# Attention that projects raw rows: the layer norm's mean in the weights, its scale in the factors, X rescaled in place

## What is computed

```python
x = x + 0.5 * ffn(layernorm(x))
a = layernorm(x)
q, k, v = split(rms_norm(a) @ w_qkv.T)
w = exp(rms_norm(k))
y = sigmoid(rms_norm(q)) * cumsum(w * v) / (cumsum(w) + 1e-6)
u, g = split(y @ w_swiglu.T)
x = x + a + (u * silu(g)) @ w_out.T
x = x + 0.5 * ffn(layernorm(x))
```

## Time and profile before

| what | us |
|---|---|
| median of 3 runs (lowest, highest) | 782.3 (782.26, 782.41) |
| span of the profiled execution | 859.9 |
| the profiled execution's time around its span | not shown by the page |
| attention, from the last shared sum to the last add_attention, in the profile | 386.5 to 508.0 |
| busy in the span: PE, DVE, ACT, POOL | 717.7, 447.1, 348.5, 427.7 |

### The profile page before, as it was taken

One profiled execution on the slowest core, in us unless ns is written; L12 is line 12 of the kernel. 1 busy time (PEld: TensorE's weight loads), 2 busy tenths in 40 slices (PEclk: granted clock), 3 DMA queues, 4 the chain that ended last, 5 costly groups with the idle time before them and its releaser, 6 DMA issues.

```text
span 859.9 us, 12865 instructions
## 1 busy us (share of the span) xinstructions
PE 717.7 (83%) x4282; PEld 591.9 (69%) x4282; DVE 447.1 (52%) x1089; ACT 348.5 (41%) x913; POOL 427.7 (50%) x499
## 2 busy tenths in 40 slices
PE   3863998988888988985887687998998988888996
PEld 3742877877776767873565475786876777777874
DVE  7689743323233333425999977953333332323437
ACT  3622622323333233445775535831333332323433
POOL 6439052465555646347898524033365656555430
PEclk9985898999999999997999997998999999999999
DMA  9600010111111111021110010001111111111128
GB/s 317 230 1 0 1 37 17 30 43 37 40 38 37 42 34 44 25 85 58 40 39 24 26 50 0 2 25 25 28 41 35 43 34 43 37 40 36 31 71 247
DMA packets 45021, 43.75 MB, mean 51 GB/s; under 512 B 5984, under 2 KB 39776, under 8 KB 44576
## 3 DMA queue, kind: packets, MB, share of 16 engines
q1 hardware_dynamic: 35872, 24.32, 9.2%
q0 software_dynamic: 9088, 18.63, 7.8%
HBM read 27.33 MB, written 15.60 MB: 50 GB/s over the span
## 4 chain that ended last, share of the span: by engine, by line
issue 40%; PE 36%; DVE 8%; ACT 3%; another core or an unknown queue 2%; DMA 1%; SPq 0%; POOL 0%; DVEq 0%; ACTq 0%
PE psY L1463 8%; PE psH L1446 4%; PE psH L1375 3%; PE psG L1306 3%; PE psG L1304 2%; PE psG L1305 2%; PE psU L1306 2%; PE psU L1304 2%; PE psU L1305 2%; DVE rec L1045 1%; PE psG L1529 1%; PE psU L1562 1%; ACT silu L1190 1%; PE psT L1403 1%
## 5 line engine op out<-in xcount | busy, mean ns | idle before, releaser
L638 POOL DMA_INDIRECT results<-yout,target x142 | 139.7, 984 | 182.3 <-DVE yout L949 144.2
L745 DVE TENSOR_TENSOR hr<-silu,psU 128x512 f32<-128x512 f32 x142 | 97.3, 685 | 252.2 <-ACT silu L1190 129.4
L623 POOL DMA_INDIRECT rows<-tokens,source x142 | 137.0, 965 | 137.8 <-issue 69.0
L1463 PE MATMUL psY<-W,hT 128*128 x1120 | 152.6, 279 | 18.2 <-issue 12.2
L1190 ACT ACTIVATE silu<-psG 128x512 f32<-128x512 f32 x142 | 85.1, 599 | 203.6 <-PE psG L1306 148.7
L1463 PEld LDWEIGHTS psY<-W,hT 128*128 128x128 f32 x1120 | 135.9, 192 | 29.6 <-issue 22.9
L1183 ACT ACTIVATE hT<-psH 128x512 f32<-128x512 f32 x142 | 84.7, 596 | 110.5 <-remote 57.2
L1446 PE MATMUL psH<-ident,hr 128*128 128x128 f32 x568 | 86.4, 275 | 26.4 <-DVE hr L745 26.4
L1446 PEld LDWEIGHTS psH<-ident,hr 128*128 128x128 f32 x568 | 68.6, 141 | 53.2 <-DVE hr L745 37.8
L745 DVE TENSOR_TENSOR hs<-silu,psU 128x512 f32<-128x512 f32 x64 | 43.4, 683 | 59.0 <-PE psU L1306 30.8
L1375 PEld LDWEIGHTS psH<-W2S,hs 128*128 128x128 f32 x512 | 65.9, 210 | 8.1 <-DVE hs L745 6.9
(11 more groups left out here) (187 smaller groups left out, 1266.1 us busy)
## 6 DMA issues: line engine op xcount, KB each, us to landing
W<-w_e SPq DMA_DIRECT2D x3, 2048.0 KB, 13.4
tokens<-XN SPq DMA_DIRECT2D x16, 256.0 KB, 3.1
Y<-results SPq DMA_DIRECT2D x32, 128.0 KB, 2.3
YF<-results SPq DMA_DIRECT2D x16, 256.0 KB, 5.1
rows<-tokens,source POOLq DMA_INDIRECT x142
results<-yout,target POOLq DMA_INDIRECT x142
X<-x SPq DMA_DIRECT2D x8, 256.0 KB, 5.6
out<-X SPq DMA_DIRECT2D x8, 256.0 KB, 2.6
```

The lines of the kernel that those rows point to most:

```text
L623: pool.indirect_dma_start(rows[:, g % RING, t, :], None, tokens, bass.IndirectOffsetOnAxis(ap=source[:, tile:tile + 1], axis=0))\
L638: pool.indirect_dma_start(results, bass.IndirectOffsetOnAxis(ap=target[:, tile:tile + 1], axis=0), yout[:, g % 2, t, :], None).then_inc(y_ ...
L745: dve.tensor_tensor(hidden, silu[:, s.u % 2, :], psU[:, s.u % 2, :], ALU.mult).then_inc(h_done, 1)
L1463: i = pe.matmul(into[:, t * D:(t + 1) * D], hT[:, s.u % 2, f, :], W2[:, bass.ds(at + f * D, D)], start=(f == 0), stop=(f == FT - 1))
```

## The change

PE transposes X itself and not `xn`. For this the qkv weights are centred once: DVE makes `centre` = identity - 1/128, PE multiplies it with WQKV into PSUM, ACT copies the product back into WQKV. The rows' scale cancels out of q and k through their norms' terms and enters v through `at_fac`. POOL's power works on eight columns; the last two give rstd, from which it makes `at_scale` = 1 + rstd and `at_shift` = mean * rstd. DVE rescales X in place (X * at_scale - at_shift = x + a), after PE's transpose of it. at_rsqrt, mean_square, residual and at_normalise are gone. The lags behind the projection fall by two.

```diff
-POOL_STAGES = [("qkv_rsqrt", 5), ("residual", 5), ("at_rsqrt", 3), ("mean_square", 4), ("add_routed", 1)]
-DVE_STAGES = [("at_normalise", 4), ("at_aggregate", 3), ("gate_g", 8), ("at_statistics", 2), ("gate_u", 8),
-              ("invert", 6), ("scale_q", 6), ("weigh_v", 5), ("attend", 6), ("add_attention", 9)]
-ACT_STAGES = [("tanh_g", 8), ("gate_results", 0), ("denominator", 6), ("copy_yT", 7), ("copy_anT", 4),
-              ("weights", 5), ("squares", 4)]
-PE_STAGES = [("cumulate", 6), ("transpose_y", 7), ("project", 9), ("transpose_xn", 4), ("qkv", 4),
-             ("swiglu", 7)]
+POOL_STAGES = [("scale_eps", 3), ("qkv_rsqrt", 3), ("add_routed", 1)]
+DVE_STAGES = [("rescale", 4), ("at_aggregate", 3), ("gate_g", 6), ("at_statistics", 2), ("gate_u", 6),
+              ("invert", 4), ("scale_q", 4), ("weigh_v", 3), ("attend", 4), ("add_attention", 7)]
+ACT_STAGES = [("tanh_g", 6), ("gate_results", 0), ("denominator", 4), ("copy_yT", 5), ("copy_xT", 2),
+              ("weights", 3), ("squares", 2)]
+PE_STAGES = [("cumulate", 4), ("transpose_y", 5), ("project", 7), ("transpose_x", 2), ("qkv", 2),
+             ("swiglu", 5)]
...
-TURNED_STEP = {20: (0, 1), 21: (2,), 22: (3,), 23: (4,), 24: (5,)}
+TURNED_STEP = {18: (0, 1), 19: (2,), 20: (3,), 21: (4,), 22: (5,)}
...
+                def scale_eps(s):
                     pool.wait_ge(at_stat, s.i + 1)
+                    u = s.u % 2
                     pool.tensor_tensor(at_eps[:, u, :, :], at_ms[:, u, 2, :].unsqueeze(1).to_broadcast([P, 2, TB]),
                                        rms_eps[:, :, :], ALU.mult).then_inc(rms_terms, 1)
...
                 def qkv_rsqrt(s):
                     pool.wait_ge(ss_done, s.i + 1)
                     pool.wait_ge(rms_terms, s.i + 1)
                     if s.past(2):
                         pool.wait_ge(kv_done, s.i - 1)
+                        pool.wait_ge(x_scaled, s.i - 1)
...
-                    pool.tensor_tensor(at_fac[:, s.u % 2, :, :], ms, minus_half[:, 0:3 * TB]
-                                       .rearrange("p (a t) -> p a t", a=3), ALU.pow).then_inc(qk_scaled, 1)
+                    pool.tensor_tensor(at_fac[:, u, :, :], ms, minus_half[:, 0:4 * TB]
+                                       .rearrange("p (a t) -> p a t", a=4), ALU.pow).then_inc(qk_scaled, 1)
+                    pool.wait_ge(qk_scaled, s.i + 1)
+                    pool.tensor_tensor(at_scale[:, u, :], at_fac[:, u, 3, :], ones[:, 0:TB], ALU.add)
+                    pool.tensor_tensor(at_shift[:, u, :], at_mv[:, u, :, 0], at_fac[:, u, 3, :], ALU.mult)\
+                        .then_inc(at_scaled, 1)
...
                 add_shared(CHUNKS - 1)
+                dve.scalar_tensor_tensor(centre[:, :], ones[:, :], -1.0 / D, ident[:, :], ALU.mult, ALU.add)\
+                   .then_inc(centre_made, 1)
...
-                def at_normalise(s):
+                def rescale(s):
                     dve.wait_ge(at_scaled, s.i + 1)
-                    if s.past(2):
-                        dve.wait_ge(anT_psum, s.i - 1)
-                        dve.wait_ge(xres_done, s.i - 1)
+                    dve.wait_ge(anT_psum, s.i + 1)
                     for t in range(TB):
...
+                        xt = X[:, s.i * TB + t, :]
+                        i = dve.tensor_scalar(xt, xt, at_scale[:, s.u, t:t + 1], at_shift[:, s.u, t:t + 1],
+                                              ALU.mult, ALU.subtract)
+                    i.then_inc(x_scaled, 1)
...
+                act.wait_ge(centred_psum, 1)
+                act.activation(WQKV[:, :], psU[:, 0, 0:3 * D], ACT.Copy).then_inc(centred, 1)
                 act_end = BATCHES + max(d for _, d in ACT_STAGES)
                 pipelined(act, [(stages[n], d) for n, d in ACT_STAGES], BATCHES, 4, straight=True,
...
+                pe.wait_ge(centre_made, 1)
+                pe.wait_ge(h_done, shared_at(0, SHARED - 1) + 1)
+                pe.matmul(psU[:, 0, 0:3 * D], centre[:, :], WQKV[:, :], start=True, stop=True)\
+                  .then_inc(centred_psum, 1)
+                pe.wait_ge(centred, 1)
...
-                    pe.wait_ge(xn_ready, s.i + 1)
+                    pe.wait_ge(routed_added, s.i + 1)
...
-                        i = pe.transpose(psT[:, t * P:(t + 1) * P], xn[:, s.u, t, :], ident[:, :])
+                        i = pe.transpose(psT[:, t * P:(t + 1) * P], X[:, s.i * TB + t, :], ident[:, :])
```

More of the change, by code:

```diff
@@ L249, in macaron @@
         at_mv = sb("at_mv", [P, 2, TB, 2])
-        at_var = sb("at_var", [P, 2, 2, TB])
-        at_rstd = sb("at_rstd", [P, 2, TB])
-        at_sq = sb("at_sq", [P, 2, TB])
+        at_scale = sb("at_scale", [P, 2, TB])
+        at_shift = sb("at_shift", [P, 2, TB])
         at_eps = sb("at_eps", [P, 2, 2, TB])
-        at_ms = sb("at_ms", [P, 2, 3, TB])
-        at_fac = sb("at_fac", [P, 2, 3, TB])
+        at_ms = sb("at_ms", [P, 2, 4, TB])
+        at_fac = sb("at_fac", [P, 2, 4, TB])
         qk_ss = sb("qk_ss", [P, 2, 2, TB])
@@ L304, in macaron @@
         memory = overlaid(
-            [("xn", [P, 2, TB, D], fp32),
+            [("centre", [P, P], fp32),
              ("anT", [P, 2, TB * P], fp32),
@@ L319, in macaron @@
             [("XNTL", [P, NT], fp32r), ("XNTH", [P, NT], fp32r)])
-        xn = memory["xn"]
+        centre = memory["centre"]
         anT = memory["anT"]
@@ L413, in macaron @@
         at_stat = sem("at_stat")
-        sq_link = sem("sq_link")
         rms_terms = sem("rms_terms")
         at_scaled = sem("at_scaled")
-        xn_ready = sem("xn_ready")
-        xres_done = sem("xres_done")
+        x_scaled = sem("x_scaled")
+        centre_made = sem("centre_made")
+        centred_psum = sem("centred_psum")
+        centred = sem("centred")
         anT_psum = sem("anT_psum")
@@ L682, in qkv_rsqrt @@
                         pool.wait_ge(kv_done, s.i - 1)
-                    ms = at_ms[:, s.u % 2, :, :]
-                    pool.tensor_tensor(ms[:, 0:2, :], qk_ss[:, s.u % 2, :, :], at_eps[:, s.u % 2, :, :], ALU.add)\
+                        pool.wait_ge(x_scaled, s.i - 1)
+                    u = s.u % 2
+                    ms = at_ms[:, u, :, :]
+                    pool.tensor_tensor(ms[:, 0:2, :], qk_ss[:, u, :, :], at_eps[:, u, :, :], ALU.add)\
                         .then_inc(qk_link, 1)
                     pool.wait_ge(qk_link, s.i + 1)
-                    pool.tensor_tensor(at_fac[:, s.u % 2, :, :], ms, minus_half[:, 0:3 * TB]
-                                       .rearrange("p (a t) -> p a t", a=3), ALU.pow).then_inc(qk_scaled, 1)
+                    pool.tensor_tensor(at_fac[:, u, :, :], ms, minus_half[:, 0:4 * TB]
[4 more added lines that the diff above has]
+                        .then_inc(at_scaled, 1)
                 if l == 0:
-                    stages = {"qkv_rsqrt": qkv_rsqrt, "add_routed": add_routed, "residual": residual,
-                              "at_rsqrt": at_rsqrt, "mean_square": mean_square}
+                    stages = {"qkv_rsqrt": qkv_rsqrt, "add_routed": add_routed, "scale_eps": scale_eps}
                     def scale_ahead(chunks):
@@ L1080, in _ @@
                 stages = {"weigh_v": weigh_v, "gate_u": gate_u, "add_attention": add_attention,
-                          "at_normalise": at_normalise, "at_statistics": at_statistics, "attend": attend,
+                          "at_statistics": at_statistics, "attend": attend, "rescale": rescale,
                           "at_aggregate": at_aggregate, "invert": invert, "scale_q": scale_q, "gate_g": gate_g}
```

45 lines of the change are left out of this document (12 added, 33 removed).

## The result

The changed kernel takes 788.5 us (median of 7 runs, 784.0 to 789.2). The kernel before, run beside it, takes 782.3 us (7 runs, 780.8 to 783.6). The ratio is 1.0068, 95% interval 1.0045 to 1.0091: slower by 5.3 us (0.0068 x 782.3; interval 3.5 to 7.1). The medians differ by 6.2, since the changed kernel's runs lie in two groups, two near 784.0 and five from 788.4 to 789.2. The forecast was 786.8, the range 781.9 to 790.0, and "slower" had 0.74. Sign and range held. The parts did not all: the start had the wrong sign, and PE's low clock in the last steps, which costs 2.4 to 4.2 us by the profiles, had no term; the two made up for each other in part.

What follows compares the result with a forecast made beforehand. DVE was taken as full in attention's middle (busy 44.0 of 45.7 us), POOL and gating as off the path. Start 1.5, lost cover 1.0 and POOL's path 2.0 gave +4.5 us: 786.8 us, range 781.9 to 790.0.

Steps and rivals of the forecast that it cites:

- (a): Start of attention: ACT's copy of the centred weights stands ahead of all gating, delaying the first transposed rows; +1.5 us.
- the second rival: Start: gating was late before too, so the change starts 3.4 us earlier; 781.9 us in all, chance 0.11.
- gating runs some 4 us ahead of need today: Start of the kernel before: ACT gates the first batches under the last shared expert, off the path.
- point of decision: Start of batch 0's gating from which late gating decides the kernel before's first transposes: 385.45, the shared sum ending at 387.16.
- (b): DVE in full steps and drain: work formerly done before the first weigh_v or under batches loses cover; +1.0 us, 0 to 3.1.
- two waits of DVE: Drain: DVE's idle ahead of rec (1.50) and an add_attention (0.48), filled by sliding layer norms; 2.0 us off.
- the last wait: Drain: DVE's 1.13 us idle ahead of the last add_attention, PE's own chain behind the last layer norm; stays.
- (c): Attention steps: ACT's weights wait for POOL's factors of the same step; +2.0 us, 0.5 in full and 1.5 in layer-norm steps.
- the port: Attention steps: DVE's ysc waits for POOL's sum into X, 0.25 us in each of 11 steps; +2.8, 789.6 us, chance 0.19.

Runs made afterwards that it cites:

- the second profile of before: The kernel before, unchanged, run once more for a profile of ordinary length: 781.24 us, span 779.4.
- PE kept busy: Changed kernel plus 28 PE products nobody reads, at the start and in idle stretches of the last steps: 782.88 us, ratio 1.0013 to before.
- the sum alone moved: Changed kernel plus an unread two-column power on POOL behind the eight-column one, so POOL's first sum into X comes later: 785.42 us, ratio 1.0041 to before.
- the power in two: Changed kernel with POOL's power split, six columns that ACT waits for, then two for the rescale: 782.98 us, ratio 1.0024 to before.
- the repairs: Changed kernel with gating first, the power in two and PE kept busy: 776.78 us, ratio 0.9931; with aggregation in the statistics' step too: 776.91 us.
- gating first: Changed kernel with ACT copying the centred weights behind the gating of three batches: 781.83 us, ratio 1.0012 to before.

## Why the prediction was right, and where it was not

**(a) The start, +1.5: the chain held, the base was wrong.** Product, copy, three gatings and first copy came as worked out (6.01 against 6.13), and the first weigh_v at 14.47 where 13.08 + 1.5 = 14.6 was forecast. But the kernel before has its own first weigh_v at 14.75 in an execution of ordinary length: its gating comes late, as the second rival said, statistics, root and normalising then stand on the path, and the change loses nothing: -0.3. The step that failed is "gating runs some 4 us ahead of need today". The doubt was written into the rival (a profile 78 us longer than a run), with a chance of 0.11; it deserved far more. Its point of decision was 0.7 us off: the starts were to be equal with gating 1.0 us ahead of the sum; at 1.4 us ahead, where the kernel before should still have won by 0.4, it lost by 0.3.

**(b) Work that lost its cover, +1.0: near it at full clock, but PE's clock had no term.** 3.1 us of DVE's work were to come out of cover, and two waits of DVE, 2.0 us in all, were to be filled. The longer of them, ahead of rec, lies ahead of the last weigh_v (450.86 in the second profile of before), so the 13.97 us of the drain before don't hold it. Timeline of that profile, DVE:

```profile
448.73 1.75 DVE L1045 RECIPROCAL rec<-den 128x256 f32<-128x256 f32 x1 [1.50 <-ACT den L1256]
```

With PE kept busy both are gone: rec at 455.00 and add_attention at 464.79 come without a wait, and only the last wait stays (1.27, before 1.13), as the prediction had it. The window from the first weigh_v to the last add_attention, in the second profile of before:

```profile
357.66:464.83 107.17, 84.39 (x405) 62.63 (x404) 100.04 (x319) 67.72 (x292) 76.54 (x131) 0.98 0.12 35
```

and in the run with PE kept busy:

```profile
355.53:466.48 110.95, 91.97 (x438) 67.09 (x438) 103.97 (x335) 70.60 (x300) 62.69 (x109) 1.00 0.14 39
```

That is 3.8 us more. Steps of the same work set side by side, (c) and the port make 2.9 of them: 1.12 in the eight full steps (5.84 against 5.70), 1.74 in the three layer-norm steps. About 0.9 is left for (b); this is a remainder of two profiles and not a run of its own. The step that failed is a term that was put at nothing: the prediction weighed PE's clock at the start alone. In the last steps PE waits for DVE, has the low clock afterwards, and then DVE waits for its last cumulations and projections. That is 1.5 to 3.3 us in the drain and 0.9 in the first step, both gone in the run with PE kept busy. In all the drain grew by 3.9 to 5.7 us. Moving the layer norms back gained nothing.

**(c) POOL on the path, +2.0: right.** From at_ms's end to weigh_v a layer-norm step shows 3.54 (timeline of the change, DVE):

```profile
442.17 0.16 DVE L1005 TENSOR_SCALAR at_ms<-at_mv 128x2 f32<-128x2 f32 x1
...
445.87 0.61 DVE L1022 SCALAR_TENSOR_TENSOR wkv<-psG,at_fac,wkv 128x128 f32<-128x128 f32 x2 [0.37 <-ACT tq L1231]
```

where 3.50 was worked out, and the power took 1.65 where 1.62 was. With ysc out of the way (the sum alone moved) the path costs 0.07 in each of eight full steps and 0.5, 0.5 and 0.7 in the layer-norm steps: 2.2. First to last weigh_v grew by 2.3, but that it is so near is chance: it also holds the port (+0.7) and the longer first step (+0.9), and one layer norm fewer, which went into the drain.

**The port.** ysc did lose to POOL's sum, at 0.98 us. The rule of the Trainium skill, "SBUF — State Buffer", section "Who interferes with whom", that whichever comes second blocks until the first is done, agrees in the direction both ways: ysc 0.98 behind the sum here, the sum 0.97 behind ysc with the power in two. The delays are a little less than a full wait: 0.56 where 0.70 of the sum was left, 0.25 where 0.39 of ysc was left. But the price was 0.08 us a step, not 0.25, because weigh_v would have waited for ACT in most of that time anyway. Two waits that end together aren't added.

**The sum.** -0.3 + 2.3 + 3.9 to 5.7 = 5.9 to 7.7 at the last add_attention (the tables' differences are 5.7 and 7.7), 4.3 to 7.5 at the first row of the next routing (131.3 before, 135.5 and 138.7 after); the runs say 5.3. Put by causes: start -0.3, path 2.2, port 0.7, lost cover 0.9, PE's clock 2.4 to 4.2. The forecast of 4.5 came near by luck: 1.8 too much at the start stood against the clock and the port, 3.1 to 4.9 that it did not have.

What stays open: why the clock falls deeper in some executions of one and the same kernel than in others, the 2.2 us between the two groups that lie ahead of attention, and why the repairs gain somewhat less together than the sum of each alone.

## What to carry to other kernels

A stage is priced against the stage of the kernel before only if that one's profile is of a usual execution: where the span is 78 us over a run, look whether the order of events at the disputed place (here the first gating against the last shared sum) is the usual one. When a shorter pipeline takes a batch's factor from the step before to the same step, the whole path to its user comes onto the ring; splitting off what the user doesn't need (six columns ahead of two) won back 2.1 us in the steps. And where a change lengthens the waits of PE in the last steps, its clock belongs into the sum: here it cost more than the work that slid into the drain.

## What the runs showed of the hardware

- PE's granted clock fell from 1.00 to 0.50 (2.4 to 1.2 GHz) after waits of 1.76 and 2.27 us in the last steps, and qkv of the first batch took 2.93 us, where it took 1.56 with PE kept busy. PE had stood idle for 3.44 us ahead of that batch's transposes; with gating first it stood idle for 1.60 us ahead of the centring product and 0.58 behind it, and that qkv still took 2.73. Products that nobody reads, put into the idle stretches, held it at 1.00 and made the changed kernel faster by 3.5 us, although they stand in PE's queue ahead of real work. The Trainium skill, "TensorE: Matmul & The Clock Gate", section "HAM oscillation — how this bites in real kernels", describes PE falling back to the slow clock in waits between groups of products; the traces agree (0.74 in the drain of the change, 1.00 with the added products).
- A power on POOL costs by its columns: 0.70 us for 2, 1.04 for 4, 1.33 for 6, 1.65 for 8. Two instructions (1.33 + 0.70) cost 0.38 more than one, and were still the faster way.
- The delay at the shared port depends on 0.04 us of order: ysc 0.83 to 0.98 when 0.03 to 0.17 us behind the sum's start, 0.43 when 0.04 ahead of it.
